# Attention's keys and values made between the stages of an earlier scan

## The reference

```
x = x + L0(x, cond)     # attention with 16 heads of 16, modulated by cond
x = x + L1(x, cond)     # scan over 128 times: Runge-Kutta of 4 stages, 256 neurons
x = x + L2(x, cond)     # transformer block, 16 heads of 128
x = x + L3(x, cond)     # scan over 128 times: GRU

# L1, one time:  i_couple = tanh(q) @ coupling.T ; dq = q - q**3/3 - p + drive + i_couple + bias   (4 times)
# L2:
x1 = ln(x) * (1 + scale1) + shift1
q, k, v = split(x1 @ qkv_w + qkv_b)             # 256 -> 3 * 2048
o = softmax(q @ k.T * 128 ** -0.5) @ v          # per sequence and head
x = x + gate1 * (o @ out_w + out_b)
x = x + gate2 * (gelu((ln(x) * (1 + scale2) + shift2) @ ffn_w1 + ffn_b1) @ ffn_w2 + ffn_b2)
```

## Time and profile before

| | us |
|---|---|
| median of 3 runs | 1871.96 (1869.98 to 1874.99) |
| the profiled execution | 1866.16 |
| its span, first to last instruction | 1864.4 |
| TensorE busy (matmul) | 1385.8 |
| VectorE busy | 1318.3 |
| ScalarE busy | 712.3 |
| GpSimd busy | 304.6 |
| first scan, first to last stage | 257.3 to 894.0 |
| attention, first matmul | 946.9 |

### The profile page before, as it was taken

One profiled execution on the slowest core, in us unless ns is written; L12 is line 12 of the kernel. 1 busy time (PEld: TensorE's weight loads), 2 busy tenths in 40 slices (PEclk: granted clock), 3 DMA queues, 4 the chain that ended last, 5 costly groups with the idle time before them and its releaser, 6 DMA issues. The chain is left out here.

```text
span 1864.4 us, 46760 instructions
## 1 busy us (share of the span) xinstructions
PE 1385.8 (74%) x16570; PEld 1089.6 (58%) x16570; DVE 1318.3 (71%) x6934; ACT 712.3 (38%) x2888; POOL 304.6 (16%) x568
## 2 busy tenths in 40 slices
PE   6898865555555545455469999999999579999975
PEld 4376633333333333333258888888888257777764
DVE  4357779999999999999665655555555446676654
ACT  4658822222222222222433434333433454444332
POOL 1025511111111111111131111111111211111110
PEclk9979975555555555555679999999999889899855
DMA  3000000000000000000210100100000130000000
GB/s 120 0 1 2 2 1 2 2 2 2 2 2 2 2 2 2 2 2 2 96 51 1 35 4 14 35 18 1 1 1 1 46 79 3 3 9 8 14 14 14
DMA packets 15201, 27.96 MB, mean 15 GB/s; under 512 B 1692, under 2 KB 9464, under 8 KB 14584
## 3 DMA queue, kind: packets, MB, share of 16 engines
q1 hardware_dynamic: 14528, 22.83, 3.7%
q0 software_dynamic: 272, 2.10, 0.6%
q10 hardware_dynamic: 168, 0.04, 0.0%
HBM read 20.77 MB, written 4.19 MB: 13 GB/s over the span
## 5 line engine op out<-in xcount | busy, mean ns | idle before, releaser
L773 PE MATMUL bank<-s_tanh_hi,coup_hi 128*128 128x16 f16 x2048 | 140.9, 179 | 317.1 <-ACT s_tanh_hi L764 317.1
L773 PEld LDWEIGHTS bank<-s_tanh_hi,coup_hi 128*128 128x128 f16 x2048 | 94.4, 107 | 364.3 <-ACT s_tanh_hi L764 364.3
L1085 ACT ACTIVATE prob<-bank,neg_max 128x128 f32<-128x128 f32 x256 | 90.7, 366 | 215.5 <-DVE neg_max L1134 215.5
L764 ACT ACTIVATE s_tanh_hi<-s_s 128x32 f16<-128x32 f32 x256 | 58.9, 230 | 231.6 <-DVE s_s L665 231.6
L773 PE MATMUL bank<-s_tanh_lo,coup_hi 128*128 128x16 f16 x2048 | 140.1, 179 | 0.8 <-DVE s_tanh_lo L660 0.2
L1199 POOL TENSOR_TENSOR prob<-prob,inv 128x512 f32<-128x512 f32 x64 | 66.7, 1042 | 426.3 <-DVE inv L1165 426.3
L773 PE MATMUL bank<-s_tanh_hi,coup_lo 128*128 128x16 f16 x2048 | 130.0, 174 | 0.0
L752 POOL TENSOR_SCALAR s_p_scaled<-s_p 128x32 f32<-128x32 f32 x128 | 37.0, 289 | 565.5 <-DVE s_p L731 544.4
L975 PE MATMUL bank<-x_hi,w_hi 128*128 128x512 f32 x256 | 111.4, 435 | 22.9 <-DVE w_lo L1114 21.2
L773 PEld LDWEIGHTS bank<-s_tanh_lo,coup_hi 128*128 128x128 f16 x2048 | 93.6, 106 | 33.5 <-DVE s_tanh_lo L660 0.7
L1415 PE MATMUL bank<-h_hi,w_h_hi 128*128 128x16 f16 x1536 | 91.2, 172 | 21.5 <-DVE h_hi L1633 21.3
(11 more groups left out here) (277 smaller groups left out, 4286.1 us busy)
## 6 DMA issues: line engine op xcount, KB each, us to landing
w_stage<-in_L_cond_qkv_w_dram SPq DMA_DIRECT2D x12, 512.0 KB, 4.9
x_tok<-in_x_dram SPq DMA_DIRECT2D x4, 512.0 KB, 5.7
ow_stage<-in_L_cond_out_w_dram SPq DMA_DIRECT2D x4, 512.0 KB, 5.4
x_in<-x SPq DMA_DIRECT2D x1, 2048.0 KB, 12.0
stage_area<-in_L_cond_ffn_w_dram SPq DMA_DIRECT2D x2, 1024.0 KB, 6.6
x<-x_in POOLq DMA_DIRECT2D x1, 2048.0 KB, 16.5
out_dram<-stage_area SPq DMA_DIRECT2D x64, 32.0 KB, 1.6
ada_w<-in_L_cond_ada_w_dram SPq DMA_DIRECT2D x1, 1536.0 KB, 12.3
```

The lines of the kernel that those rows point to most:

```text
L764: A.activation(th_hi[:, :], s, ACT.Tanh, scale=scale).then_inc(hi_ready, 1)
L773: ins = nc.tensor.matmul(coupled[:, B * m:B * m + B], w[:, o:o + P], th[:, B * c:B * c + B], start=(first and c == 0 and m == 0), stop=(la ...
L1085: last = A.activation(prob[:, grp % 2, h, :], bank[2 + grp % 2][:, T * h:T * h + T], ACT.Exp, bias=neg_max[:, grp % 2, h:h + 1], accum_out ...
```

## The change

The last 32 times of L1 apart, a block of 32 finished times (512 columns of all sequences) is normalised, modulated, split and projected to keys and values while the scan goes on. That is done for blocks 0 to 2 inside `scan1`, one piece behind or ahead of the work of a stage. `piece(i)` on each engine says what belongs to stage `i`; with r the stage in the following block of 128:

- VectorE, ahead of the state write: low parts of the weights (64 pieces of 128 columns in the stages 24 to 55 and 76 to 107 of the first block), then per block sums (r 0 to 7), centring (8 to 15), scaling (24 to 31), low part (36 to 43).
- TensorE, behind a stage's products: means (r 2, 4, 6, 8), variances (18 to 21), and from r 45 on 32 tiles of 6 matmuls of 512 columns, half a tile per stage.
- ScalarE, behind the stage's two tanh: high parts of the weights, squares (16, 17), Ln and Exp (22), modulation, high part, and the evacuation of a tile every second stage.
- SyncE stores each tile (128 x 512 fp32, 256 KB) to DRAM from a ring of five.

The last block has a phase of its own, `finish_kv`, in the place of `norm_split`: the same for 32 times, then 32 tiles one behind the other, evacuated by ScalarE and VectorE in turns. `attend2` projects q alone (4 products a unit, one a slot), loads keys and values of a unit (1 MB each, four DMAs each) from DRAM, and adds the values' bias on VectorE. Where `scan1` summed all times at its end, nothing is left there. The diff, cut to its core:

```diff
+KV_EARLY = 3
+RING = 5
+W_AT, SCALED_AT, LOW_AT, TILES_AT = (20, 72), 24, 36, 45
...
+def kv_products(nc, g, out, n, i, lo, hi, full):
+
+    hg, k = divmod(i, 8)
+    for m in range(lo, hi):
+        c, w = divmod(m, 3)
+        x_hi, x_lo = g.x_hi(c, n), g.x_lo(c, n)
+        if k < 4:
+            cols = slice(512 * hg + D2 * k, 512 * hg + D2 * k + D2)
+            stat, mov = (g.wkv_h[:, 0, c, cols], g.wkv_l[:, 0, c, cols]), (x_hi, x_lo)
+        else:
+            toks, cols = slice(128 * (k - 4), 128 * (k - 4) + 128), slice(512 * hg, 512 * hg + 512)
+            stat, mov = (x_hi[:, toks], x_lo[:, toks]), (g.wkv_h[:, 1, c, cols], g.wkv_l[:, 1, c, cols])
+        ins = nc.tensor.matmul(out, stat[w == 2], mov[w == 1], start=(m == 0), stop=(m == 5))
+    if hi == 6:
+        ins.then_inc(full, 1)
...
+        @block.sync
+        def _(sp):
+            w = a["L2_cond_qkv_w"].rearrange("(c p) n -> p c n", p=P)
+            for part in range(2):
+                o = H2 * D2 * (part + 1)
+                if part:
+                    sp.wait_ge(wl_ready, 32)
+                sp.dma_start(w_raw, w[:, :, o:o + H2 * D2]).then_inc(d_wkv[part], 16)
+            for n in range(KV_EARLY):
+                for i in range(2 * H2):
+                    u = 2 * H2 * n + i
+                    sp.wait_ge(tile_out, u + 1)
+                    sp.dma_start(kv_tile(g, n, i), stage[:, u % RING, :]).then_inc(d_tile[u % RING], 16)
+            load_w2(sp, a, g, 0)
+            load_ow(sp, a, g, 0)
+            load_vb(sp, a, g, 0)
...
+            def centre(n, k, c):
+                dve.wait_ge(mean_full, 4 * n + 4)
+                V.tensor_tensor(xc[:, c, quarter(k)].rearrange("p (b t) -> p b t", t=TB),
+                                g.x2[:, c, 4 * k:4 * k + 4, times(n)],
+                                MEAN[:, quarter(k)].rearrange("p (b t) -> p b t", t=TB), SUB).then_inc(xc_ready, 1)
...
+            def piece(i):
+                for part in range(2):
+                    if W_AT[part] + 4 <= i < W_AT[part] + 36:
+                        w_low(32 * part + i - W_AT[part] - 4)
+                n, r = divmod(i - 4 * TB, 4 * TB)
+                if n >= 0:
+                    k, c = r // 2 % 4, r % 2
+                    if r < 8:
+                        sums(n, k, c)
+                    elif r < 16:
+                        centre(n, k, c)
+                    elif SCALED_AT <= r < SCALED_AT + 8:
+                        scaled(n, k, c)
+                    elif LOW_AT <= r < LOW_AT + 8:
+                        x_low(n, (r - LOW_AT) % 4, (r - LOW_AT) // 4)
...
                 def advance(stage, out, scale, n):
+                    piece(4 * j + stage - 1)
                     dve.wait_ge(coupled_ready, 4 * j + stage)
...
-            for c in range(C):
-                V.tensor_tensor(g.x2[:, c, :, :], g.x1[:, :, c, :].rearrange("p t b -> p b t"),
-                                g.trace[:, 1:T + 1, c, :].rearrange("p t b -> p b t"), ADD)
...
+            def evacuate(n, i):
+                u = 2 * H2 * n + i
+                act.wait_ge(tile_full, u + 1)
+                if u >= RING:
+                    act.wait_ge(d_tile[u % RING], 16 * (u // RING))
...
+                elif r == 22:
+                    act.wait_ge(var_full, 4 * n + 4)
+                    A.activation(log_var[:, :], VAR[:, :], ACT.Ln, bias=g.eps6[:, :]).then_inc(log_ready, 1)
+                    act.wait_ge(log_ready, n + 1)
+                    A.activation(rstd[:, :], log_var[:, :], ACT.Exp, scale=-0.5).then_inc(rstd_ready, 1)
...
+            def half_tile(n, i, half):
+                u = 2 * H2 * n + i
+                if half == 0:
+                    if u >= 5:
+                        pe.wait_ge(tile_out, u - 4)
+                    if i == 0:
+                        pe.wait_ge(xl_ready, 8 * n + 8)
+                        pe.wait_ge(wl_ready, 64)
+                kv_products(nc, g, TILE_BANK[u % 5][:, :], n, i, 3 * half, 3 * half + 3, tile_full)
+
+            def piece(i):
+                n, r = divmod(i - 4 * TB, 4 * TB)
+                if n < 0:
+                    return
+                if r in (2, 4, 6, 8):
+                    k = r // 2 - 1
+                    pe.wait_ge(x2_ready, 8 * n + C * k + C)
+                    average(MEAN, lambda c: g.x2[:, c, 4 * k:4 * k + 4, times(n)], k, mean_full)
+                elif r in (18, 19, 20, 21):
+                    k = r - 18
+                    pe.wait_ge(sq_ready, C * n + C)
+                    average(VAR, lambda c: square[:, c, quarter(k)], k, var_full)
+                elif TILES_AT <= r < TILES_AT + 4 * H2:
+                    half_tile(n, *divmod(r - TILES_AT, 2))
+
             for i in range(4 * T):
                 pe.wait_ge(hi_ready, i + 1)
                 product(g.coup_hi, th_hi, True, False)
                 product(g.coup_lo, th_hi, False, False)
                 pe.wait_ge(lo_ready, i + 1)
                 product(g.coup_hi, th_lo, False, True).then_inc(coupled_ready, 1)
+                piece(i)
...
+def finish_kv(nc, ctx, a, g):
...
+            for i in range(TILES):
+                sp.wait_ge(tile_out[i % 2], i // 2 + 1)
+                sp.dma_start(kv_tile(g, n, i), stage[:, i % RING, :]).then_inc(d_tile[i % RING], 16)
...
+            pe.wait_ge(xl_ready, 2 * C)
+            for i in range(TILES):
+                if i < 2:
+                    pe.wait_ge(log_ready, 2)
+                if i >= 5:
+                    pe.wait_ge(tile_out[(i - 5) % 2], (i - 5) // 2 + 1)
+                kv_products(nc, g, bank[3 + i % 5][:, :], n, i, 0, 6, tile_full)
...
-def attend2(nc, ctx, a, g, xh, xl):
+def attend2(nc, ctx, a, g):
...
-    STEPS = 12
...
+    STEPS = 4
...
+            for u in range(UNITS):
+                hg, bg = divmod(u, 4)
+                if u >= 2:
+                    sp.wait_ge(s_full, 4 * (u - 1))
+                for n in range(4):
+                    keys = g.k_dram[n, HG * hg:HG * hg + HG].rearrange("h d (b t) -> d h b t", b=B)
+                    sp.dma_start(k2[:, u % 2, :, n, :, :].rearrange("p h b t -> p h (b t)"),
+                                 keys[:, :, BB * bg:BB * bg + BB, :].rearrange("d h b t -> d h (b t)")).then_inc(d_k[u % 2], 16)
+                if u >= 2:
+                    sp.wait_ge(o_full, 4 * (u - 1))
+                for n in range(4):
+                    values = g.v_dram[n, bg].rearrange("(b t) c -> t b c", b=BB)
+                    sp.dma_start(v2[TB * n:TB * n + TB, u % 2, :, :],
+                                 values[:, :, 512 * hg:512 * hg + 512]).then_inc(d_v[u % 2], 16)
+                if bg == 1 and hg + 1 < HG:
+                    sp.wait_ge(wl_ready, hg + 1)
+                    load_w2(sp, a, g, hg + 1)
+                    sp.wait_ge(owl_ready, hg + 1)
+                    load_ow(sp, a, g, hg + 1)
+                    load_vb(sp, a, g, hg + 1)
...
-                w, j = divmod(s, 4)
-                pe.wait_ge(wl_ready, 3 * hg + w + 1)
+                pe.wait_ge(wl_ready, hg + 1)
                 if i >= 2:
-                    proj_evacuated(pe, i - 2)
-                parts = []
-                for c in range(C):
-                    if w < 2:
-                        cols, toks = slice(D2 * j, D2 * j + D2), slice(512 * bg, 512 * bg + 512)
-                        parts.append((w_h[:, w, c, cols], w_l[:, w, c, cols], xh[:, c, toks], xl[:, c, toks]))
-                    else:
-                        t0 = 512 * bg + T * j
-                        parts.append((xh[:, c, t0:t0 + T], xl[:, c, t0:t0 + T], w_h[:, w, c, :], w_l[:, w, c, :]))
-                three(bank[i % 2][:, :], parts, proj_full)
+                    pe.wait_ge(q_out, i - 1)
+                cols = slice(D2 * s, D2 * s + D2)
+                three(bank[i % 2][:, :], [(w_h[:, c, cols], w_l[:, c, cols], g.x_group(g.x_hi_all, c, bg),
+                                           g.x_group(g.x_lo_all, c, bg)) for c in range(C)], proj_full)
...
-                    pe.wait_ge(kv_out, 8 * u + 4)
+                    pe.wait_ge(d_k[u % 2], 64 * (u // 2 + 1))
...
+                if 0 <= grp < GROUPS:
+                    u = p - 1
+                    dve.wait_ge(g.d_vb[u // 4], 16)
+                    dve.wait_ge(d_v[u % 2], 64 * (u // 2 + 1))
+                    V.tensor_tensor(v2[:, u % 2, k, :], v2[:, u % 2, k, :], g.v_bias[:, (u // 4) % 2, :],
+                                    ADD).then_inc(v_out, 1)
...
+            with ExitStack() as early:
+                g.wkv_h = sb(early, "wkv_hi", [P, 2, C, H2 * D2], F32R)
+                g.wkv_l = sb(early, "wkv_lo", [P, 2, C, H2 * D2], F32R)
+                g.trace = sb(early, "trace", [P, T + 1, C, B])
+                with ExitStack() as ctx:
+                    scan1(nc, ctx, a, g)
+                with ExitStack() as ctx:
+                    finish_kv(nc, ctx, a, g)
             with ExitStack() as ctx:
-                scan1(nc, ctx, a, g)
```

(62 more changed lines are left out.)

280 lines of the change are left out of this document (207 added, 73 removed).

## The result

The changed kernel takes 1755.01 us (median of 4 runs, 1752.01 to 1756.03), the kernel before 1872.22 in the same comparison: a ratio of 0.9371, 95% interval 0.9359 to 0.9382. The forecast was 1760. The profiled executions have spans of 1864.43 and 1753.95 us, 110.5 less.

| stretch | before | after | change | forecast |
|---|---|---|---|---|
| up to the scan's first state write | 258.84 | 261.76 | +2.9 | 0 |
| scan, first to last state write | 634.78 | 670.55 | +35.8 | +40 |
| to attention's first matmul | 53.27 | 75.77 | +22.5 | +17 |
| attention, its first to its last weight matmul | 509.06 | 339.48 | -169.6 | -170 |
| to the second scan's first matmul | 82.45 | 82.25 | -0.2 | 0 |

What follows compares the result with a forecast made beforehand. The prediction took a ring between engines to bound the first scan and TensorE to bound attention. Scan +40, between +17 and attention -170 gave -113 on 1866.2, 1753; with 5.8 for the median, 1760, range 1730 to 1812.

Steps and rivals of the forecast that it cites:

- Attention -170: Attention: 128 key and value products gone at 1.37 us, -175, plus 5 for softmax lag: -170 us.
- softmax's ring: Attention: the softmax chain is late next once projections go; +0.3 us per unit, +5, ends 0 and +40.
- about 4.0: Attention slots without output product: softmax chain 4.0 us against TensorE's 3.6, repaid in slots with one.
- The clock: Scan's tile stages: full clock after a low start, projections then cost nothing; +6 us, ends -3 and 100.
- cold stages: Tile stages at the low clock: four at each block's start, 0.52 us longer each, three times, 6 us.
- VectorE's pieces: Scan: 160 instructions ahead of state writes, 13.6 us plus 5.0 for sums; together 19, ends 0 and 45.
- Stalls: Scan: stage 8's centring wait 3.3 us, mean and variance matmuls 2.4, Ln and Exp with table loads 9.0.
- Between scan and attention: From the scan's end to attention's first matmul: 70 us instead of 52.7, +17; ends +10 and +40.
- 2 for attention's first weights: Between scan and attention: 2 us for attention's first weights, part of the 70 us.
- Clock low throughout: Rival: the clock stays low in the scan's tile stages, 192 x 0.52 us, total 1854; chance 0.08.
- Stores: Rival: tile stores hold the scan and the kernel gets slower, 1923 us at 3.5 us per 256 KB; chance 0.04.
- The ring: Rival: in attention the softmax chain takes TensorE's place, lag not repaid, 34 us, total 1794; chance 0.17.

Runs made afterwards that it cites:

- q_thin: Changed kernel without two of the three partial products of each q projection (4 of 6 matmuls, 64 times): 1735.76 us.
- fill4: Changed kernel with a fourth matmul added to the three in each of the scan's 192 tile stages: 1776.58 us.
- thin: Changed kernel without five of the six matmuls of each key and value tile made in the scan: 1755.36 us.
- centre_later: Changed kernel with a block's first centring and all that follows it one stage later, averages left in place: 1752.35 us.
- spread: Changed kernel with ScalarE's scaling and shift two to a stage over 16 stages instead of four over eight: 1749.23 us.
- add_late: Changed kernel with GpSimd's two additions at attention's start waiting until both pairs of VectorE's weight remainders are made: 1750.26 us.
- stores_twice: Changed kernel with each of the scan's 96 tiles stored twice, a buffer being free when both have landed: 1752.97 us.

## Why the prediction was right

The forecast was 1760 and the time 1755. On the profiled execution the sum was -113 us against -110.5, so its 1753 was 3 us too low (1756.03). The forecast comes out above the time only because it added 5.8 us, by which the median of before lay above the profiled execution; in the changed kernel the median lies 1.0 below it. By its own steps:

- *Attention -170.* Measured -169.6. 128 products at full clock went, and TensorE stayed at 257.8 of 260 us. That the number fits so closely is luck in part. 5.8 us of the 175.4 did not come, but not for softmax's ring, to which the prediction gave +5: TensorE waits for normalised rows in attention's last pass alone, as before. About 2.9 go with a low clock at attention's end, where it was 0.50 from 1337.05 to 1343.88 us; five variants without that stretch took 336.5 to 336.8 us instead of 339.5. Another 1.8 are waits of the scores for ScalarE's evacuation of q (3.5 us of waits for q in all, where there were 1.7 before). The prediction's 31 us a unit are also not four of its slots of 7.54; they are the trace's steady unit, 31.2, of which 20.4 are left for its 20.2. The ring is there all the same: "about 4.0" a slot without output product is 3.93 in the row maxima, while TensorE needs 3.61 (its scores started at 1156.38 and 1159.99). The 0.3 was repaid in the slots with output product, as forecast. q_thin shows what the profile hides: one more cut on TensorE and the ring decides, 20 to 22.5 us for 58 of matmuls.
- *The clock.* Right, and the premise of the sum: low in block 0, where VectorE's pieces but no fills run, and full in 78.5 us of each block. The cold stages were two or three at 1.81 where four at 1.75 were forecast; with the warm ones 0.02 shorter, the tile stages cost 2.4 us against 6. Their cover was larger than priced: fill4 paid 0.10 a stage for a matmul of 0.23. The scan gets hardly anything else from the full clock: thin, without it, is 1.7 us shorter.
- *VectorE's pieces.* The 64 weight remainders 5.6 us (block 0, 163.35 against 157.79) for a forecast of 6.4; sums with averages, stages 0 to 7, 4.4 for 6.2; low parts 2.2 for 2.4.
- *Stalls.* Centring's stages 4.8 for 5.7, and centre_later gave back 3.4 for 3.3. The prediction's terms for stage 8 (0.86, 0.2, 0.2) add up to 1.26, though, and not to its 1.1, and the stage did take 1.27 more than before; centre_later gave back less than that, since stages 9 and 16 grew by 0.09 and 0.15. Stages 16 to 23, with Ln, Exp and variances, 10.1 for 10.2; the load ends at 458.02 and Ln starts at 458.03, so nothing stands between them, as in the earlier trace rows.
- *Missed: scaling and shift.* The prediction priced their stages by VectorE's piece alone and gave ScalarE's four instructions of 32 columns no term. Stages 24 to 35 cost 6.0 us for 2.4, and spread gave 3.2 of it back. The Trainium skill (ScalarE: Activation LUTs, What ACT_TABLE_LOAD costs) gives by estimate 0.40 us for one with two pointer operands and, since neighbours overlap by 0.09, 1.32 for four; the trace has 1.31. ScalarE's idling was 0.92.
- *Between scan and attention.* +22.5 for +17. First tile matmul 19.2 us behind the sums' start for 18, the tiles 46.5 for 46.3. The failing term is "2 for attention's first weights": it was 5.4 from block change to first matmul, and add_late shows why, by 3.4. The same pairing stood in the trace of before, three remainders in 8.72 us beside the additions, and I had not read it as contention:

```profile
942.13 8.72 DVE L1114 TENSOR_TENSOR w_lo<-w_stage,w_hi 128x512 fp32r<-128x512 f32 x3 [0.46 <-ACT w_hi L1064]
942.24 8.06 POOL L1195 TENSOR_TENSOR x<-x,gate_b 128x2048 f32<-128x2048 f32 x2
```

- *The rivals.* Clock low throughout: out by the trace. Stores: out by stores_twice. The ring: real, but hidden by TensorE's output products.

The scan's misses (3.6 too little for scaling and shift, 3.6 too much for the tiles, 3.8 for pieces and stalls) cancelled in part; the sum is better than its terms.

## What to carry to other kernels

Work put into the gaps of a chain is free only up to the gap of each engine it passes through, and in queues that are in order it is paid in front of the very next link: price each piece on every engine it uses, not only on the busiest. Then read the wait of the late part (here the product behind VectorE) as further room. And before an offload to GpSimd, ask what VectorE does meanwhile: an idle engine is not free room if its work slows another's, as GpSimd's did VectorE's here.
